# A recurrent cell with an error input: error rows from transposed predictions, and the second cell's hidden state in one operation

## The reference

```python
encoded = tanh(xt @ We + st @ Ue + be)                       # 24 numbers
new_state = tanh(einsum('bd,cds->bcs', xt, Wx) + einsum('bs,cst->bct', st, Ws) + bk)
inp = concatenate([encoded, err[:, None]], axis=1)           # 25 numbers
mem = concatenate([inp[:, None, :], mem[:, :-1, :]], axis=1) # the last 20
a = relu(mem.reshape(b, -1) @ enc_w1 + enc_b1)
agent_in = relu(a @ enc_w2 + enc_b2)
h1, c1 = lstm_cell(agent_in, h1, c1, ...)
h2, c2 = lstm_cell(h1, h2, c2, ...)
gate = softmax(h2 @ gate_w + gate_b, axis=1)
theta = clamp01(mean(abs(mem[:, :10, -1]), axis=1) * 2.5)[:, None]
gate = gate * theta + gs * (1.0 - theta)
st = einsum('bc,bcs->bs', gate, new_state)
pred = clamp01(st[:, -1])                                    # the output
err = pred - yt
```

## Time and profile before

| | |
|---|---|
| median of 3 runs | 5459.47 us (5458.23 to 5461.18) |
| profiled execution, its own time | 5460.57 us |
| its span in the trace | 5458.7 us |
| PE busy | 5391.8 us (99%) |
| PEld busy | 3426.0 us (63%) |
| DVE busy | 4479.8 us (82%) |
| ACT busy | 3807.2 us (70%) |
| POOL busy | 2421.7 us (44%) |
| mean granted TensorE clock | 0.998 |

### The profile page before, as it was taken

One profiled execution on the slowest core, in us unless ns is written; L12 is line 12 of the kernel. 1 busy time (PEld: TensorE's weight loads), 2 busy tenths in 40 slices (PEclk: granted clock), 3 DMA queues, 4 the chain that ended last, 5 costly groups with the idle time before them and its releaser, 6 DMA issues.

```text
span 5458.7 us, 188210 instructions
## 1 busy us (share of the span) xinstructions
PE 5391.8 (99%) x67584; PEld 3426.0 (63%) x67584; DVE 4479.8 (82%) x12336; ACT 3807.2 (70%) x9729; POOL 2421.7 (44%) x4613
## 2 busy tenths in 40 slices
PE   8999999999999999999999999999999999999998
PEld 5666666666666666666666666666666666666665
DVE  7888888888888888888888888888888888888887
ACT  5777777777767777777777777777777777777775
POOL 3444444444444444444444444444444444444444
PEclk9999999999999999999999999999999999999999
DMA  2111111111111111111111111111111111111111
GB/s 69 29 29 32 29 32 29 32 29 32 29 32 29 32 29 30 31 29 32 29 32 29 32 29 32 29 32 29 30 31 29 32 29 32 29 32 29 32 29 40
DMA packets 299285, 172.38 MB, mean 32 GB/s; under 512 B 156734, under 2 KB 263882, under 8 KB 298714
## 3 DMA queue, kind: packets, MB, share of 16 engines
q1 hardware_dynamic: 293568, 159.42, 11.2%
q10 hardware_dynamic: 5146, 3.66, 0.2%
HBM read 74.65 MB, written 2.10 MB: 14 GB/s over the span
## 4 chain that ended last, share of the span: by engine, by line
PE 95%; DVE 4%; issue 1%; DMA 0%; POOL 0%; ACT 0%; DVEq 0%; ACTq 0%; POOLq 0%
PE a_ps L366 26%; PE chain L417 17%; PE cand_ps L338 9%; PE a_ps L377 9%; PE cand_ps L347 7%; PE chain L310 5%; PE chain L317 4%; PE chain L403 4%; PE chain L293 4%; PE a_ps L388 3%; PE chain L435 3%; PE cand_ps L330 3%; DVE mixed L799 1%; DVE state L817 1%; DVE added L720 1%
## 5 line engine op out<-in xcount | busy, mean ns | idle before, releaser
L366 PE MATMUL a_ps<-hist,w_hist 125*64 125x512 f16 x12288 | 1896.3, 383 | 24.1 <-DMA w_hist<-enc_table 24.1
L817 DVE TENSOR_REDUCE state<-mixed 128x64 f32<-128x512 f32 x2048 | 1353.4, 682 | 34.2 <-POOL mixed L920 0.8
L920 POOL TENSOR_TENSOR mixed<-cand,gate 128x512 f32<-128x512 f32 x1024 | 1281.1, 1272 | 48.6 <-POOL gate L908 12.5
L554 ACT ACTIVATE cand<-cand_ps 128x512 f32<-128x512 f32 x2048 | 1101.8, 593 | 91.1 <-PE cand_ps L347 90.6
L417 PE MATMUL chain<-cell_in,cell_w 128*64 128x128 f32 x16384 | 1120.7, 278 | 19.8 <-DVE cell_in L735 19.8
L886 POOL TENSOR_TENSOR one_theta<-ones,theta 128x8 f32<-128x8 f32 x512 | 103.4, 202 | 2241.0 <-DVE theta L702 2241.0
L417 PEld LDWEIGHTS chain<-cell_in,cell_w 128*64 128x64 f32 x16384 | 889.2, 136 | 271.5 <-DVE cell_in L735 211.8
L366 PEld LDWEIGHTS a_ps<-hist,w_hist 125*64 125x64 f16 x12288 | 681.4, 109 | 536.2 <-issue 141.7
L561 ACT ACTIVATE gates<-chain 128x384 f32<-128x384 f32 x1024 | 502.0, 490 | 726.3 <-PE chain L417 726.1
L735 DVE SCALAR_TENSOR_TENSOR cell_in<-gates,tanh_c 64x128 f32<-64x128 f32 x2048 | 582.5, 284 | 127.0 <-ACT tanh_c L571 113.4
L720 DVE SCALAR_TENSOR_TENSOR added<-gates 128x256 f32<-128x256 f32 x1024 | 537.1, 524 | 141.2 <-ACT gates L561 141.2
(11 more groups left out here) (76 smaller groups left out, 6823.8 us busy)
## 6 DMA issues: line engine op xcount, KB each, us to landing
x_sb<-in_x_l SPq DMA_DIRECT2D x260, 256.0 KB, 2.7
hist<-entry_parts SPq DMA_DIRECT2D x2048, 25.0 KB
w_hist<-enc_table SPq DMA_DIRECT2D x258, 128.0 KB, 2.4
y_rows<-in_y_l SPq DMA_DIRECT2D x260, 8.0 KB
ys<-in_y ACTq DMA_DIRECT2D x1, 2048.0 KB, 16.3
preds_out<-preds SPq DMA_DIRECT2D x1, 2048.0 KB, 7.5
cand<-in_encoder ACTq DMA_DIRECT2D x1, 640.0 KB, 3.8
cell_w<-in_cell ACTq DMA_DIRECT2D x2, 256.0 KB, 4.5
```

The costliest lines, as they stand in the source:

```text
L366: nc.tensor.matmul(a_ps[g][ENC * half:ENC * half + ENC, :], w_hist[0:HROWS, w_slot(u), kk, wp, :], hist[0:HROWS, xp, k, at:at + 512], star ...
L554: ins = nc.scalar.activation(cand[:, g, q // 2, :, q % 2, :, :].rearrange("p h s c -> p h (s c)"), cand_ps[q][:, :].rearrange("p (h k) -> ...
L817: V.tensor_reduce(state[:, g, hf, 2 * pair:2 * pair + 2, :], mixed[:, pair, hf, :, :, :], AX, ALU.add)\
L920: G.tensor_tensor(mixed[:, 0, :, q, :, :], cand[:, g, 0, :, q, :, :], over_s, ALU.mult)\
```

## The change

The prediction is computed right after the sums of the state and laid out by halves. Two transposes of its 4 columns each (`prediction_transpose`) put it into rows 0 to 3 of `cand_ps[0]`, and `errors` subtracts y from there; ScalarE's `at_least_zero` goes. `w_ue` loses its four copying columns, and `encoded_s` goes over three strips of 32 columns in place of 64 and 36; `encoded_x` over four strips of 32. Cell 1's hidden state is one VectorE operation of 128 partitions into `h_second`. `gate_logits` reads that with two matmuls of 64 moving columns, and `keep_hidden` makes two copies into `cell_in[1]` for the next step's `cell_gates(cur, 1)`, which waits for them. `errors` stands ahead of cell 1's hidden state on VectorE. On the tensor engine the history pieces stand in other places.

```diff
-ENTRY_ROWS = (slice(0, HALF), slice(HALF, ER))
+ENTRY_ROWS = tuple(slice(S * r, S * r + S) for r in range(ZR // S))
+CHAIN_ROWS = tuple(slice(S * r, S * r + S) for r in range(P // S))
...
+            def prediction_transpose(item):
+                g, n, u = item
+                pe.wait_ge(q_pred, n)
+                pe.wait_ge(q_cand[0], n)
+                for hf in range(HF):
+                    last = nc.tensor.matmul(cand_ps[0][0:Q, P * hf:P * hf + P],
+                                            pred_now[:, g, Q * hf:Q * hf + Q], ident[:, :], is_transpose=True, start=True, stop=True,
+                                            skip_group_check=True)
+                last.then_inc(q_predps, 1)
...
-                for rows in ENTRY_ROWS:
+                for rows in CHAIN_ROWS:
                     nc.tensor.matmul(chain[g][rows, Z_AT:Z_AT + COLS], w_we[:, rows], x_sb[:, x_slot(u), g, :],
...
-                    pe.wait_ge(q_rl, n)
+                    pe.wait_ge(q_err, n)
...
                 else:
+                    pe.wait_ge(q_hkept, n)
                     pe.wait_ge(q_h[0], n)
...
-                for hf in range(HF):
-                    for rows in CELL0_OUT:
-                        last = nc.tensor.matmul(chain[g][rows, 0:TILES * C]
-                                                .rearrange("p (a h k) -> p a h k", a=2, h=HF)[:, :, hf, :],
-                                                cell_in[1][:, g, hf, rows], gate_w[:, hf, :],
-                                                start=False, stop=True, skip_group_check=True)
+                for rows in CELL0_OUT:
+                    last = nc.tensor.matmul(chain[g][rows, 0:TILES * C], h_second[:, g, rows], gate_w[:, :],
+                                            start=False, stop=True, skip_group_check=True)
...
                     history(cur, 2, 1, 3)
-                    history(cur, 3, 0, 1)
+                    prediction_transpose(cur)
                     encoded_s(cur)
                 if new:
                     history_waits(new, extra)
                     history(new, 0, 0, 1)
                 if cur:
-                    history(cur, 3, 1, 2)
+                    history(cur, 3, 0, 1)
                 if old:
                     logit_bias(old)
-                if new:
-                    history(new, 0, 1, 2)
-                if old:
                     gate_logits(old)
                 if cur:
-                    history(cur, 3, 2, 3)
+                    history(cur, 3, 1, 3)
                     encoder1_now(cur)
                     bias_of_cell(cur, 0)
                 if new:
-                    history(new, 0, 2, 3)
-                    history(new, 1, 0, 2)
+                    history(new, 0, 1, 3)
                 if cur:
                     encoder2(cur)
+                if cur:
                     candidates_bias(cur)
                 if new:
-                    history(new, 1, 2, 3)
+                    history(new, 1)
...
-            def at_least_zero(item):
-                g, n, u = item
-                act.wait_ge(q_zps, n)
-                nc.scalar.activation(clamped[ZR:ER, g, :], chain[g][ZR:ER, Z_AT:Z_AT + COLS], ACT.Relu)\
-                    .then_inc(q_rl, 1)
...
-                dve.wait_ge(q_rl, n)
-                V.scalar_tensor_tensor(entry[ZR:ER, g, :], clamped[ZR:ER, g, :], 1.0,
-                                       y_rows[ZR:ER, x_slot(u), g, :], ALU.min, ALU.subtract)\
+                dve.wait_ge(q_predps, n)
+                V.tensor_tensor(entry[ZR:ER, g, :], cand_ps[0][0:Q, 0:COLS], y_rows[0:Q, x_slot(u), g, :],
+                                ALU.subtract)\
                     .then_inc(q_err, 1)
...
+            def second_hidden(item):
+                g, n, u = item
+                dve.wait_ge(q_tanhc[1], n)
+                dve.wait_ge(q_out_gate[1], n)
+                V.scalar_tensor_tensor(h_second[:, g, :], gates[1][:, g, 0, :], 1.0, tanh_c[1][:, g, :],
+                                       ALU.add, ALU.mult).then_inc(q_h[1], 1)
+
+            def keep_hidden(item):
+                g, n, u = item
+                dve.wait_ge(q_h[1], n)
+                for hf in range(HF):
+                    rows = CELL1_OUT[hf]
+                    last = V.tensor_copy(cell_in[1][rows, g, hf, :], h_second[rows, g, :])
+                last.then_inc(q_hkept, 1)
...
                     mix_sum(old, 1, 1)
+                    prediction(old)
                 if cur:
                     error_sum(cur)
                     cell_terms(cur, 1)
...
                     cell_value(cur, 1)
+                if new:
+                    errors(new)
+                if cur:
+                    second_hidden(cur)
                     thetas(cur)
-                if old:
-                    prediction(old)
-                if cur:
-                    new_hidden(cur, 1, 0)
-                    new_hidden(cur, 1, 1)
-                if new:
-                    errors(new)
-                if cur:
                     peaks(cur)
                     below_peak(cur)
+                    keep_hidden(cur)
                     totals(cur)
```

More of the change, by code:

```diff
@@ L61, in recurrent_kernel @@
         ones16 = sb("ones16", [P, P], FP16)
-        w_we = sb("w_we", [P, ER])
-        w_ue = sb("w_ue", [P, ER])
+        w_we = sb("w_we", [P, P])
+        w_ue = sb("w_ue", [P, ZR])
         w_x = sb("w_x", [P, NS])
@@ L132, in recurrent_kernel @@
         s_hist = [sem(f"s_hist_group{g}") for g in range(GROUPS)]
-        (q_trps, q_st, q_zps, q_enc, q_rl, q_err, q_eh, q_el, q_aps, q_a, q_inps, q_in,
+        (q_trps, q_st, q_zps, q_enc, q_predps, q_err, q_eh, q_el, q_aps, q_a, q_inps, q_in,
          q_candps) = (
-            sem(f"q_{n}") for n in ("trps", "st", "zps", "enc", "rl", "err", "eh", "el", "aps", "a",
+            sem(f"q_{n}") for n in ("trps", "st", "zps", "enc", "predps", "err", "eh", "el", "aps", "a",
                                     "inps", "in", "candps"))
@@ L151, in recurrent_kernel @@
         q_in_high = sem("q_in_high")
+        q_hkept = sem("q_hkept")
         q_sum = [[sem(f"q_sum{hf}_{pair}") for pair in range(2)] for hf in range(HF)]
@@ L599, in phase @@
                 if new:
-                    at_least_zero(new)
                     encoded(new)
@@ L683, in _ @@
             dve.wait_ge(s_y[0], 16)
-            first = y_rows[ZR:ER, 0, :, :].rearrange("p g b -> p (g b)")
+            first = y_rows[0:Q, 0, :, :].rearrange("p g b -> p (g b)")
             link(V.tensor_scalar(first, first, -1.0, None, ALU.mult))
@@ L727, in cell_value, with first_hidden @@
                                        added[c][:, g, 0, :], ALU.mult, ALU.add).then_inc(q_cell[c], 1)
-            def new_hidden(item, c, hf):
+            def first_hidden(item, hf):
                 g, n, u = item
[L731 to L738, removed]
+                rows = CELL0_OUT[hf]
+                if hf == 0:
+                    dve.wait_ge(q_tanhc[0], n)
+                    dve.wait_ge(q_out_gate[0], n)
+                last = V.scalar_tensor_tensor(cell_in[1][rows, g, hf, :], gates[0][rows, g, 0, :], 1.0,
+                                              tanh_c[0][rows, g, :], ALU.add, ALU.mult)
+                if hf == HF - 1:
+                    last.then_inc(q_h[0], 1)
+            def second_hidden(item):
[11 more added lines that the diff above has]
+                last.then_inc(q_hkept, 1)
             def agent_input(item, hf):
@@ L824, in prediction @@
                         dve.wait_ge(q_sum[hf][pair], n + GROUPS)
-                V.tensor_scalar(pred_now[:, g, :].rearrange("p (a h l) -> p a h l", a=2, h=HF),
-                                state[:, g, :, :, S - 1].rearrange("p h (a l) -> p a h l", a=2),
+                V.tensor_scalar(pred_now[:, g, :].rearrange("p (h q) -> p h q", h=HF), state[:, g, :, :, S - 1],
                                 1.0, 0.0, ALU.min, ALU.max).then_inc(q_pred, 1)
@@ L847, in phase @@
                 if cur:
-                    new_hidden(cur, 0, 0)
-                    new_hidden(cur, 0, 1)
+                    first_hidden(cur, 0)
+                    first_hidden(cur, 1)
                 if old:
@@ L943, in new_error @@
                 step, ring = place(item, extra)
-                pool.wait_ge(q_pred, n)
+                pool.wait_ge(q_pred, n + GROUPS)
                 pool.wait_ge(q_errsum, n)
-                pred = pred_now[:, g, :].rearrange("p (j o) -> p j o", o=1)
-                G.tensor_tensor(err_ring[:, tiles, bass.ds(ring, 1)], pred, ys[:, tiles, bass.ds(step, 1)],
-                                ALU.subtract).then_inc(q_ring, 1)
+                pred = pred_now[:, g, :].rearrange("p (h a l) -> p a h l", h=HF, a=2)
+                G.tensor_tensor(by_quarter(err_ring[:, tiles, bass.ds(ring, 1)]), pred,
+                                by_quarter(ys[:, tiles, bass.ds(step, 1)]), ALU.subtract).then_inc(q_ring, 1)
```

(13 more changed lines are left out.)

22 lines of the change are left out of this document (12 added, 10 removed).

## The result

5845.7 us (median of 4, 5842.2 to 5850.5) against 5458.9 before: ratio 1.071, interval 1.069 to 1.073. The direction was right, the size was not: 387 us slower where 233 were forecast, above the range.

A forecast was written before the change was run, and what follows sets the result against it. PE was taken as the bound, full and at the edge of each wait. Terms 0.05 - 0.01 + 0.385 + 0.03 = 0.455 us a phase, times 512 = 233 us on 5460.6, gave 5694 us, range 5580 to 5790.

The forecast's parts named there:

- 512 items of that are nearly the whole span: PE's timeline: one phase takes 10.53 us, and 512 of them make up nearly all the time.
- Sum: Whole kernel: 0.455 us more a phase, times 512 = 233 us, to 5694 us.
- Up to encoder1_now: PE from a phase's first history group to encoder1_now: start at 3.12 us in place of 3.07, +0.05.
- rival 2: New transposes cost 0.46 as ordinary products, 5770 us; or full-array shape with one more change, 0.10 a phase; chance 0.14.
- The tie at the logits: Ahead of the logits: cell 1's h lets them start at 2.56 us, PE's own stream arrives at 2.54.
- encoder1_now to encoder2: PE stretch with two history pairs left of three: ScalarE's relu sets encoder2's start, PE waits 0.21; -0.01 us.
- encoder2 to the gates: PE from encoder2 to cell 0's gates: three history pairs in place of one, 1.325 us against 0.94, +0.385.
- Mode changes at 0.10: PE: each change of the shape in which the array is cut costs about 0.10 us, lower end 0.
- Rival 1: Strips beside halves cost nothing on PE: 0.285 us a phase, 5607 us; chance 0.18.
- To cell 1's gates: PE, encoded_x over four strips: +0.10 for a change to halves, 0.08 of waiting mostly hidden; +0.03 us.
- 0.16 to 0.29 each: keep_hidden's two copies ahead of totals, reckoned hidden where VectorE sits idle 0.58 us for the exponentials.
- Rival 3 (faster): The error chain paces the phase; without the relu encoder1_now starts earlier, phase 10.48 us, 5435 us; chance 0.06.

The follow-up runs named there:

- the run with halves: Changed kernel with encoded_s and encoded_x in two halves of 64 stationary columns in place of strips of 32: 5589.2 us, ratio 1.024.
- the run with a third pair: Changed kernel with encoded_s and encoded_x in halves, and one history pair moved from behind encoder2 to ahead of it: 5519.7 us, ratio 1.011.
- the run with the hidden state alone: Kernel before with only second_hidden, keep_hidden's copies and the two-matmul gate_logits of the change: 5535.2 us, ratio 1.013.
- the fastest run: Kernel before with second_hidden, two-matmul gate_logits, keep_hidden's copies on ScalarE, waits moved, and encoded_s one history pair earlier: 5408.5 us, ratio 0.991.

## Why the prediction was wrong

- **The step that failed is "512 items of that are nearly the whole span"**, taken over into "Sum" as 0.455 x 512 and nothing else. The cost once a turn had no term; it came to some 170 us. The change put 100 instructions into a turn of 2753, which moved the closing branch from slot 193 of one block to slot 37 of the next. Moving only the loop's head took 161 and 170 us off the changed kernel and put 217 us on the kernel before. That the branch is the place is shown, and so is what it waits for; why the same slot 37 costs the kernel before only 50 us, that is why its fetch starts 1.8 us earlier, is not explained.
- **The phase** came near its forecast, 10.95 against 10.98, in part by luck: its parts missed by -0.05 to +0.06 and nearly cancelled. Two reliefs weren't in the sum: cell 0's gates to the candidates' x takes 0.97 in place of 1.02 (probably the agent's input, which the prediction called early and priced at nothing), and cell 1's gates 0.88 in place of 0.92.
- **"Up to encoder1_now", +0.05**: 2720.70 - 2717.52 = 3.18 against 3.07, +0.11. The new transposes take 0.31 to the next group, reckoned 0.29, and ran as one instruction each, so rival 2's 0.46 did not happen. Its other form, the shape of the full array with one more change, isn't excluded: the transposes take the same 0.31 whether strips follow them or halves (2712.39 to 2712.70 in the run with halves). The rule of the Trainium skill, "TensorEngine Tiling (Array Packing)", section "Feature Incompatibilities", that column tiling and FP32 transpose mode exclude each other on TRN2, is thus neither borne out nor refuted here. The tie at the logits was not one: h ended at 2719.91 and the logits started at 2720.12, so PE's own stream set the start.
- **encoder1_now to encoder2, -0.01**: 2722.52 - 2720.70 = 1.82 against 1.88, with the wait of 0.2 in it, and the run with a third pair shows it to be idle time. **encoder2 to the gates, +0.385**: 2723.87 - 2722.52 = 1.35 against 0.94, +0.41. This was the largest term, and it was right.
- **Mode changes at 0.10**: history to the transposes 0.56 for two pairs, 0.13 over streaming; strips to halves 0.08 to 0.09, with their additional instructions. Rival 1, that strips beside halves are free, fell with the run with halves.
- **To cell 1's gates, +0.03**: encoded_x to the gates 0.81 against 0.76, +0.05; the gates themselves 0.88 against 0.92.
- **The copies "0.16 to 0.29 each"** average 0.45, but that is a mean of two kinds: one of the pair takes 0.23, inside the estimate, the other 0.67, because it waits for a GpSimd operation (last section). What was missing is the wait. On PE it doesn't show in the changed kernel, where cell 0's h is there 0.26 us ahead of cell 1's gates; in the run with the hidden state alone it did.
- **Rival 3 (faster)** did not come: in the changed kernel encoder1_now starts 1.10 us after the error rows and 0.47 after the tanh, so neither paces it. Its premise, that this chain paces encoder1_now, is what the fastest run lives on.

## What to carry to other kernels

A sum over the steady phase is not the time: when an edit adds instructions to a loop's body, count them against the blocks in which code is fetched, and look at how long the closing branch takes; then try the same code at another place before judging the edit. Compare two versions only when both branches are cheap, or the layout of code is what gets measured. On an engine that is full and at the edge of every wait, a filler moved from ahead of a wait to behind it saves nothing where it leaves, since a hole takes its place, and costs its length where it lands. Here moving one pair of 0.22 us back gained 0.14 a phase.

## What the hardware showed that was not expected

- A waiting branch ended 1.36 to 1.52 us after the packet of its instruction fetch, in 200 of 200 turns of four runs; the packet itself took 0.9 to 1.5 us.
- A stop of about 3 us at the branch can lower TensorE's clock to 1.2 GHz for 3.4 or 6.8 us behind it: in 20 of 50 turns of the changed kernel, 1.8 us a turn, some 36 us in all, and in 41 of 50 turns of the kernel before with its head at 64. Behind the stops of the branch of 1.4 us (head at 100) there was no drop in 50 turns. One stall has two prices. Its length alone doesn't decide: idle times of PE from 2.4 to 2.9 us came with a drop and without.
- A VectorE copy of 64x128 fp32 takes 0.22 us alone and 0.60 (0.67 in the changed kernel) where GpSimd's 0.67 us operation (line 941 here) had started first. In the run with the hidden state alone:

```profile
2709.93 0.84 DVE L752 COPY cell_in<-h_second 64x128 f32<-64x128 f32 x2
```

```profile
2710.01 0.67 POOL L941 TENSOR_TENSOR entry_parts<-entry,entry_parts 128x256 f16<-128x256 f32 x1 [0.57 <-ACT entry_parts L530]
```

  The first copy is over at 2710.15. The second ends at 2710.77, 0.08 us after the GpSimd operation, and so it does in 511 phases (0.076 to 0.083), and the long one in 501 phases of the changed kernel (0.077 to 0.087). The copy waits for the whole operation; it isn't merely slowed. The mean of 0.45 that the changed kernel's page gives hides this. `cell_terms`, with its 0.28 us after the mix, behaves alike.
- Of two waits ahead of one matmul, the answer to the one written first came 0.05 us after the result, to the other 0.14: the trace has the second as an instruction of its own of 0.05 us ahead of the matmul. So the order in which waits are written can be worth 0.09 a phase.
